# Two fp16 weight parts under a scale computed on the chip, one semaphore for both scan inputs, and a first step without recurrent passes, in a two-LSTM kernel

## The reference

```
def lstm(x, h0, Wx, Wh, b):            # _L0_cond_ref and _L0_cond2_ref, c0 = 0
    xp = einsum('ntd,df->ntf', x, Wx) + b
    for t in range(128):
        a = xp[:, t] + h @ Wh                       # 16 x 512
        i, f, o = sigmoid(a[:, :H]), sigmoid(a[:, H:2H]), sigmoid(a[:, 2H:3H])
        g = tanh(a[:, 3H:])
        c = f * c + i * g
        h = o * tanh(c)                             # kept for every t
attn(y)  = ((y Wtheta^T)(y Wphi^T)^T / sqrt(128)) (y Wg^T)     # linear, no softmax
x = x + attn(lstm(x, cond, Wx1, Wh1, b1))
x = x + relu(lstm(x, cond, Wx2, Wh2, b2) W1 + bb1) W2 + bb2
```

## Time and profile before

| | us |
|---|---|
| median of three runs | 469.54 (469.51 to 469.75) |
| the profiled execution, its own time | 466.24 |
| its span, first to last instruction | 464.2 |
| busy: TensorE / VectorE / ScalarE / GpSimd | 441.4 / 261.0 / 212.0 / 17.1 |

### The profile page before, as it was taken

The page is one execution under the profiler, slowest core; times in us unless marked ns, Lnnn a source line. Parts: engine busy times, 40 slices in busy tenths (PEclk is TensorE's granted clock), DMA queues, the critical chain, the costliest instruction groups (busy, mean ns, idle before and its releaser), DMA issues.

```text
span 464.2 us, 17097 instructions
## 1 busy us (share of the span) xinstructions
PE 441.4 (95%) x6350; PEld 351.3 (76%) x6440; DVE 261.0 (56%) x1422; ACT 212.0 (46%) x1092; POOL 17.1 (4%) x29
## 2 busy tenths in 40 slices
PE   7999999999999999999999999999999999999997
PEld 5877777777777777777789977777777777777775
DVE  4455555555555555555545656556656656665664
ACT  1444455554455555445535344444444444444443
POOL 6800000000000000000000000000000000000000
PEclk9999999999999999999999999999999999999999
DMA  5001111100111110010000000000000000000000
GB/s 168 7 3 18 17 17 17 17 12 5 17 17 17 17 17 9 8 17 11 11 13 3 7 20 20 17 17 14 3 17 17 17 17 17 11 6 17 17 17 11
DMA packets 11689, 8.12 MB, mean 17 GB/s; under 512 B 1097, under 2 KB 11129, under 8 KB 11674
## 3 DMA queue, kind: packets, MB, share of 16 engines
q1 hardware_dynamic: 10874, 6.17, 6.7%
q0 software_dynamic: 512, 1.22, 0.8%
q10 hardware_dynamic: 288, 0.52, 0.3%
HBM read 2.87 MB, written 1.05 MB: 8 GB/s over the span
## 4 chain that ended last, share of the span: by engine, by line
PE 75%; DVE 11%; ACT 9%; issue 3%; DMA 1%; ACTq 0%; DVEq 0%
PE fobank L389 19%; PE gibank L379 16%; PE fobank L379 9%; DVE cell L752 6%; ACT scan L667 5%; DVE ring L755 4%; ACT cell L674 4%; PE gibank L354 3%; PE gibank L359 3%; PE fobank L354 3%; PE fobank L359 3%; PE bankV L365 2%; PE bankY L533 2%; PE bankV L443 2%; PE bankU L526 2%
## 5 line engine op out<-in xcount | busy, mean ns | idle before, releaser
L389 PEld LDWEIGHTS fobank<-ring,whf 128*128 128x128 f32 x510 | 76.6, 189 | 77.8 <-DVE ring L755 70.3
L664 ACT ACTIVATE fgate<-fobank 128x16 f32<-128x16 f32 x256 | 46.9, 183 | 165.0 <-PE fobank L389 162.7
L389 PE MATMUL fobank<-ring,whf 128*128 128x16 f32 x510 | 99.8, 271 | 15.1 <-DVE ring L755 13.1
L748 DVE TENSOR_TENSOR scan<-fgate,cell 128x16 f32<-128x16 f32 x256 | 45.3, 177 | 86.8 <-ACT fgate L664 84.7
L752 DVE TENSOR_TENSOR_SCAN cell<-scan 128x48 f32<-128x48 f32 x256 | 68.4, 267 | 36.8 <-ACT scan L667 1.3
L379 PEld LDWEIGHTS gibank<-h_hi,wh_parts 128*128 128x128 bf16 x1536 | 78.9, 110 | 0.0
L755 DVE SCALAR_TENSOR_TENSOR ring<-cell,ogate 128x16 f32<-128x16 f32 x256 | 44.6, 174 | 59.9 <-ACT cell L674 59.9
L379 PE MATMUL gibank<-h_lo,wh_parts 128*128 128x16 f16 x1536 | 75.3, 169 | 0.3 <-DVE h_lo L760 0.2
L379 PE MATMUL gibank<-h_hi,wh_parts 128*128 128x16 f16 x1536 | 75.4, 169 | 0.0
L667 ACT ACTIVATE scan<-gibank 128x32 f32<-128x32 f32 x256 | 54.8, 214 | 28.7 <-PE gibank L379 0.8
L379 PE MATMUL fobank<-h_hi,wh_parts 128*128 128x16 f16 x771 | 60.0, 174 | 0.4 <-ACT fgate L664 0.2
(11 more groups left out here) (150 smaller groups left out, 463.2 us busy)
## 6 DMA issues: line engine op xcount, KB each, us to landing
rows_t<-rows SPq DMA_DIRECT2D x16, 128.0 KB
x_rows<-in_x_dram SPq DMA_DIRECT2D x17, 64.0 KB
out_dram<-y_sb SPq DMA_DIRECT2D x16, 64.0 KB
xres<-x2T SPq DMA_DIRECT2D x15, 64.0 KB, 1.9
xin<-x2T SPq DMA_DIRECT2D x14, 64.0 KB, 1.8
w<-in_L_ffn_W_dram POOLq DMA_DIRECT2D x2, 256.0 KB, 3.9
wh<-in_L_cond_Wh_dram ACTq DMA_DIRECT2D x1, 256.0 KB, 2.8
wx<-in_L_cond_Wx_dram ACTq DMA_DIRECT2D x1, 256.0 KB, 3.8
```

The source lines that it names most:

```text
L389: nc.tensor.matmul(step_out(p, t, GF), whf[layer][:], ring[:, (s - 1) % STEPS, :], start=False, stop=True, skip_group_check=True).then_inc ...
L664: nc.scalar.activation(fgate[:], fobank[p][:, NB * t:NB * t + NB], ACT.Sigmoid).then_inc(f_done[layer], 1)
L748: nc.vector.tensor_tensor(out=fc_slots, in0=fgate[:], in1=c_psum, op=ALU.mult).then_inc(fc_done[layer], 1)
```

## The change

- `passes` runs over **two** float16 parts of Wh instead of three bfloat16 parts: 4 passes a gate instead of 6.
- So that they fit float16's exponents, Wh is divided by a power of two and multiplied by 2^13. The power of two is found on the chip from the largest |Wh|: VectorE reduces each partition's row, TensorE spreads the 128 maxima to all partitions by a product with a diagonal matrix, VectorE takes the maximum and keeps its exponent bits. It yields four values a layer in `scale[layer]`, one column each.
- All of PSUM's pre-activations therefore carry this factor and H_UNIT: x, the bias (or the ones beside it) and h0 are multiplied by it beforehand, and ScalarE takes it out again: the scale of the three gate activations is now a column of `scale[layer]` (a 128 x 1 tile) where it was a constant.
- ScalarE's tanh of g and i and VectorE's fgate * c both count on one semaphore, `scan_inputs`, and the scan waits once, for 2n + 2.
- Step 0 of each layer has no recurrent passes: `initial` (layer 1) and `project_gate` (layer 2) signal f_ready, gi_ready and o_ready themselves. Layer 1's first 16 steps are now written out and its loop is Fori(1, ITER).
- Layer 2's scale is made between the steps of layer 1: VectorE after steps 8, 9 and 12, TensorE after step 12. GpSimd then scales wx, bias, h0 of layer 2 and splits Wh in four instructions (before: six).

```diff
-        wh_parts = [sb(f"wh_parts{n}", [P, 3, 4 * H], bf16) for n in (1, 2)]
+        wh_parts = [sb(f"wh_parts{n}", [P, 2, 4 * H], f16) for n in (1, 2)]
...
             if layer == 0:
-                e.scalar_tensor_tensor(out=rest[:], in0=w[:], scalar=1.0 / H_UNIT, in1=parts[:, 0, :],
+                eng.wait_ge(done, 2)
+                e.scalar_tensor_tensor(out=parts[:, 1, :], in0=w[:], scalar=w_scale(layer), in1=parts[:, 0, :],
                                        op0=ALU.mult, op1=ALU.subtract).then_inc(done, 1)
             else:
...
-            eng.wait_ge(done, 3 + layer)
-            e.tensor_copy(parts[:, 1, :], rest[:]).then_inc(done, 1)
-            eng.wait_ge(done, 4 + layer)
-            e.tensor_tensor(out=parts[:, 2, :], in0=rest[:], in1=parts[:, 1, :], op=ALU.subtract).then_inc(done, 1)
...
+            def top_product(layer, out):
+                pe.wait_ge(scale_made[layer], 2)
+                nc.tensor.matmul(out, ones[:], w_diag[:], start=True, stop=True).then_inc(top_ready[layer], 1)
...
                     for g in gs:
-                        for part in range(3):
+                        for part in range(2):
...
-            nc.tensor.matmul(bankV[:, 0:2 * P], warm_w[:], zeros[:], start=True, stop=True, skip_group_check=True)
-            pe.wait_ge(bias_ready, 1)
-            for g in GATES:
-                bias_gate(0, 0, g)
             pe.wait_ge(cond_loaded, 16)
             nc.tensor.transpose(bankY[:, 0:NB], cond_rows[:], ident[0:NB, 0:NB]).then_inc(cond_transposed, 1)
-            pe.wait_ge(xT_kept, 1)
-            pe.wait_ge(wx_ready, 1)
-            for g in GATES:
-                project_gate(0, 0, g, xT[:, 0, :])
+            keep_warm(bankV, 2)
+            top_product(0, gibank[1][:, 0:P])
             pe.wait_ge(h0_kept, 1)
-            pe.wait_ge(wh_ready, 1)
-            initial(0)
-
             pe.wait_ge(attn_w_loaded, 48)
             nc.tensor.matmul(bankY[:, 0:P], wtp[:, 1, :], wtp[:, 0, :], start=True, stop=True)
             nc.tensor.matmul(bankY[:, 2 * P:3 * P], wtp[:, 0, :], wtp[:, 1, :], start=True, stop=True)
             nc.tensor.transpose(bankY[:, P:2 * P], wg_rows[:], ident[:]).then_inc(proj_ready, 1)
-            pe.wait_ge(parts_ready[0], 5)
+            nc.tensor.matmul(bankV[:, 0:2 * P], warm_w[:], zeros[:], start=True, stop=True, skip_group_check=True)
+            pe.wait_ge(bias_ready, 1)
+            pe.wait_ge(ones_z_ready, 1)
+            for g in GATES[0:3]:
+                bias_gate(0, 0, g)
+                if g == GF:
+                    pe.wait_ge(xT_kept, 1)
+                    pe.wait_ge(wx_ready, 1)
+                project_gate(0, 0, g, xT[:, 0, :])
+                if g == GF:
+                    pe.wait_ge(h0_ready, 1)
+                    pe.wait_ge(wh_ready, 1)
+                last = initial(0, g)
+                if g == GF:
+                    last.then_inc(f_ready[0], 1)
+            last.then_inc(gi_ready[0], 1)
+            pe.wait_ge(f_done[0], 1)
+            bias_gate(0, 0, GO)
+            project_gate(0, 0, GO, xT[:, 0, :])
+            initial(0, GO).then_inc(o_ready[0], 1)
...
+            for s in range(STEPS):
+                if s > 0:
+                    if s == 1:
+                        pe.wait_ge(parts_ready[0], PARTS[0])
+                    step(0, s, s)
+                if s == 13:
+                    pe.wait_ge(scale_made[1], 3)
+                beside1(0, s)
+                if s == 12:
+                    top_product(1, bankU[:, 2 * P:3 * P])
+            with pe.Fori(1, ITER) as i:
...
-            for g in GATES:
-                last = project_gate(1, 0, g, x2T[:, 0, :])
-            last.then_inc(x2_projected, 1)
-            pe.wait_ge(parts_ready[1], 6)
+            project_gate(1, 0, GF, x2T[:, 0, :]).then_inc(f_ready[1], 1)
+            project_gate(1, 0, GG, x2T[:, 0, :])
+            project_gate(1, 0, GI, x2T[:, 0, :]).then_inc(gi_ready[1], 1)
+            pe.wait_ge(f_done[1], 1)
+            project_gate(1, 0, GO, x2T[:, 0, :]).then_inc(o_ready[1], 1)
...
                 nc.scalar.activation(fgate[:], fobank[p][:, NB * t:NB * t + NB],
-                                     ACT.Sigmoid).then_inc(f_done[layer], 1)
+                                     ACT.Sigmoid, scale=z_of(layer)).then_inc(f_done[layer], 1)
...
-                                     ACT.Tanh, scale=0.5).then_inc(gi_done[layer], 1)
+                                     ACT.Tanh, scale=z_half(layer)).then_inc(scan_inputs[layer], 1)
...
-                                     ACT.Sigmoid).then_inc(tanh_done[layer], 1)
+                                     ACT.Sigmoid, scale=z_of(layer)).then_inc(tanh_done[layer], 1)
...
                 nc.vector.tensor_tensor(out=fc_slots, in0=fgate[:], in1=c_psum,
-                                        op=ALU.mult).then_inc(fc_done[layer], 1)
-                dve.wait_ge(gi_done[layer], n1)
-                dve.wait_ge(fc_done[layer], n1)
+                                        op=ALU.mult).then_inc(scan_inputs[layer], 1)
+                dve.wait_ge(scan_inputs[layer], n * 2 + 2)
...
+            def most_of(layer, loaded):
+                dve.wait_ge(loaded, 16)
+                nc.vector.tensor_reduce(w_most[layer][:], wh[layer][:], axis=mybir.AxisListType.X, op=ALU.max,
+                                        apply_absolute_value=True).then_inc(scale_made[layer], 1)
+            def spread_most(layer):
+                dve.wait_ge(scale_made[layer], 1)
+                nc.vector.tensor_scalar(w_diag[:], ident[:], w_most[layer][:], LEAST, ALU.mult,
+                                        ALU.max).then_inc(scale_made[layer], 1)
+            def scale_from(layer, top):
+                dve.wait_ge(top_ready[layer], 1)
+                nc.vector.tensor_reduce(w_top[:], top, axis=mybir.AxisListType.X, op=ALU.max
+                                        ).then_inc(scale_made[layer], 1)
+                ...   # and with the exponent mask, times units, xor, times units: four instructions on 1 to 2 columns
...
+            for s in range(STEPS):
+                step(0, s, s)
+                beside1(0, s)
+                if s == 8:
+                    most_of(1, wh2_loaded)
+                if s == 9:
+                    spread_most(1)
+                if s == 12:
+                    scale_from(1, bankU[:, 2 * P:3 * P])
```

More of the change, by code:

```diff
@@ L201, in build, with z_of, z_half, w_scale @@
         out_tb = out.rearrange("b (c t) d -> c t b d", t=CH)
+        def z_of(layer):
+            return scale[layer][:, 0:1]
+        def z_half(layer):
+            return scale[layer][:, 1:2]
+        def w_scale(layer):
+            return scale[layer][:, 2:3]
+        def x_scale(layer):
+            return scale[layer][:, 3:4]
         def split_wh(eng, e, layer):
-            done, w, parts, rest = parts_ready[layer], wh[layer], wh_parts[layer], wh_rest[layer]
-            e.tensor_scalar(whf[layer][:], w[:, gate_cols(GF)], 1.0 / H_UNIT, None, ALU.mult).then_inc(done, 1)
@@ L211, in split_wh @@
                                        op0=ALU.mult, op1=ALU.subtract).then_inc(done, 1)
             else:
[L213 removed]
+                e.tensor_scalar(wh_rest[:], w[:], w_scale(layer), None, ALU.mult).then_inc(done, 1)
                 eng.wait_ge(done, 3)
[L215 to L216 removed]
@@ L217, in split_wh @@
-            e.tensor_copy(parts[:, 1, :], rest[:]).then_inc(done, 1)
-            eng.wait_ge(done, 4 + layer)
-            e.tensor_tensor(out=parts[:, 2, :], in0=rest[:], in1=parts[:, 1, :], op=ALU.subtract).then_inc(done, 1)
-        def start_h(layer):
-            nc.vector.memset(h_hi[:, STEPS - 1, :], 0.0).then_inc(hi_ready[layer], 1)
-            nc.vector.memset(h_lo[:, STEPS - 1, :], 0.0).then_inc(lo_ready[layer], 1)
+                e.tensor_tensor(out=parts[:, 1, :], in0=wh_rest[:], in1=parts[:, 0, :],
+                                op=ALU.subtract).then_inc(done, 1)
@@ L225, in start_h, with clear_c, at @@
+        PARTS = [3, 4]
+        def clear_c(layer):
             nc.vector.memset(c_psum, 0.0).then_inc(c_cleared, 1)
             nc.vector.wait_ge(c_cleared, layer + 1)
+        def at(eng, value):
+            return value if isinstance(value, int) else eng.snap(value)
         @block.sync
@@ L352, in bias_gate @@
             def bias_gate(layer, p, g):
-                return nc.tensor.matmul(gate_out(p, g), bias[layer][:, gate_cols(g)], moving(ones[:, :], g),
+                return nc.tensor.matmul(gate_out(p, g), bias[layer][:, gate_cols(g)],
+                                        moving((ones_z, ones)[layer][:, :], g),
                                         start=g in (GF, GG), stop=False, skip_group_check=True)
```

255 lines of the change are left out of this document (158 added, 97 removed).

## The result

The changed kernel takes 549.62 us (median of four runs, 548.56 to 566.81), the kernel before 469.52 (468.03 to 469.75, four runs beside them): a ratio of 1.1706 [1.1669, 1.1744]. All ratios, with 95% intervals in brackets, are made from the executions within 1.5% of the fastest of their kernel, here without the one of 566.81. I had written 467.2. The profiled execution took 550.2 us, its span 548.1, against 464.2 before.

The account below looks back on a forecast made before the run. No engine is full; the step is pure latency. Steady steps -2.6, TensorE-bound steps +0.4, layer 2's step 0 -0.5, start -0.2, layer 2's scale +0.6 sum to -2.3: 469.54 becomes 467.2 us, range 463.5 to 475.

Parts of the forecast that it names:

- rival C: TensorE's clock falls with six passes fewer a step; ten steps at the lower level cost about 5 us; chance 0.05.
- second mark: Sign of a fallen TensorE clock in the trace: the passes would start 0.05 us apart.
- GpSimd's part: GpSimd's preparation of layer 2's weights during layer 1: claimed to have 200 us of cover.
- One semaphore: 0: The scan's wait: two waits cost no more than one, so merging gains 0; bound 0.04 us a step.
- My 11 ns a step: Steady steps: 100 ns from fewer passes less 89 for the column; 237 steps give -2.6 us.
- Passes: TensorE's passes for g and i: 12 become 8, so their gates come 0.100 us earlier a step; alone 23.7 us.
- Column: ScalarE's gate activations: a column as scale instead of a constant costs 89 ns, between 0 and twice 89.
- Rival A: ScalarE's scale column is free, so the whole 0.100 us a step comes through: 445 us; chance 0.10.
- Handover: Layer 2's step 0, now without recurrent passes: its tanh of g and i starts earlier, -0.5 us.
- TensorE-bound steps: About ten steps early in layer 2, where TensorE is the bound: each 0.04 us longer, +0.4 us.
- layer 2's scale inside layer 1: VectorE's reductions and waits between layer 1's steps: +0.6 us, between 0.2 and 1.5.
- The start: Layer 1's step 0 with scale making and reordered input products: -0.2 us, between -1.5 and +2.

Follow-up runs that it names:

- 11: Changed kernel with three passes a gate again (second part used twice) in layer 2's first 16 steps alone: 470.5 us.
- 16: Changed kernel with the fill in layer 1's first 16 steps alone: 548.47 us.
- 10: Changed kernel with the fill everywhere but in layer 2's first 16 steps: 469.14 us.
- experiment 4: Kernel before with a 128 x 1 column as scale of its three gate activations, all passes kept: 495.86 us.
- 3: Kernel before with its third bfloat16 part left out of the passes, constants as scales: 460.42 us.
- 15: Changed kernel with constants as the three gate scales, nothing else added: 441.61 us.
- Experiment 5: Changed kernel with the fill in TensorE's pause before gate o's passes in every step, added into columns nothing reads: 463.07 us.
- 2: Changed kernel with three passes a gate again in every step, the second part used twice: 488.29 us.
- 6: Changed kernel with the fill in every step and two semaphores before the scan again: 479.28 us.
- 9: Changed kernel with the fill in layer 2's first 16 steps alone: seen twice, 466.95 and 536.8 us.
- 13: Changed kernel with the fill in layer 2's first 16 steps alone, timed again in more rounds: 470.52 us.
- experiment 12: Kernel before with one merged semaphore for both scan inputs: 464.12 us.
- the fill: Two extra TensorE products of 256 columns on constants, which nothing waits for, added to the changed kernel; in every step, 463.07 us.
- experiment 7: Changed kernel with the fill in every step and constants as the three gate scales, right for these weights alone: 442.86 us.
- 14: Changed kernel with the fill in every step, placed behind gate o's passes instead of in the pause before them: 465.38 us.
- 8: Changed kernel with the fill in the first 16 steps of each layer alone, none in the loops: 465.1 us.

## Why the prediction was wrong

**The step that failed is rival C, its chance and its price.** The mechanism was named, with the right mark to look for (a granted clock under 1.00), and put at 0.05 and ten steps. Its second mark, passes 0.05 apart, is not in the trace: the 16-column passes start 0.027 us apart at the lower level and 0.025 at the higher, and it is the 128-column products that go from 0.11 to 0.21. Measured: 11 steps at the lower level in layer 1, near what ten were priced at (+6.3), and then all of the last 117, +78.7, which I didn't consider. Two sentences carried the mistake.

- "The passes removed are 16 columns each, very little of the array's work." Experiments 11 and 16 are the same in layer 2 but for those passes in 15 steps, and 11 holds where 16 falls. That a granted clock of 1.00 over the whole record left a margin was assumed; no row said how large it was, and a row of 1.00 can't.
- "If the lower of the two levels (1.2 GHz) held for ten steps it would cost about 10 x 0.5 = 5 us". It was priced as an episode, and at 0.5 us a step, where the row it quotes (2.46 against 1.70) gives 0.76 and 0.67 was measured. At the lower level the recurrent step is bound by TensorE, 2.36 instead of 1.69 us, so the same products are spread over 40% more time; that a recovery must follow was never argued. In layer 1 it followed after 24 us. In the kernel before it always did: of its 68 executions timed beside the experiments, 26 have a mean clock of 0.996 or less (0.996 is some 3.7 us at the lower level), the lowest 0.95, and none takes over 482 us. The one trace at 1.00 that I read was of an execution without such a dip. In layer 2 only extra work brought it (10) or the third passes, which experiment 4 still has.

**What starts the fall** is narrowed down for layer 2, though on two executions for most of the kernels: it is the first 16 steps, through the six passes fewer each and the longer ScalarE instructions together. Each alone only dips (3 and 4), and with constant scales (15) the level of layer 2 holds even without the passes. In layer 1 it is less sharp. The level fell at 46.3, after the steps 13, 14 and 18 had each grown. Timeline of the changed kernel around step 13:

```profile
33.94 0.29 DVE L836 TENSOR_REDUCE w_top<-bankU 128x1 f32<-128x128 f32 x1
...
34.78 0.23 DVE L847 TENSOR_SCALAR scale<-units,w_inv 128x2 f32<-128x2 f32 x1
34.92 0.17 DVE L872 TENSOR_TENSOR scan<-fgate,cell 128x16 f32<-128x16 f32 x1
...
35.87 0.28 PE L434 MATMUL fobank<-ring,whf 128*128 128x16 f32 x1 [0.55 <-DVE ring L878]
...
36.83 0.57 DVE L875 TENSOR_TENSOR_SCAN cell<-scan 128x48 f32<-128x48 f32 x1
...
42.46 1.15 POOL L251 TENSOR_TENSOR wh_parts<-wh_rest,wh_parts 128x512 f16<-128x512 f32 x1
...
43.16 0.48 DVE L883 TENSOR_TENSOR h_lo<-ring,h_hi 128x16 f16<-128x16 f32 x1
```

VectorE's reduction and the four small ones hold fgate * c back, and TensorE waits 0.55 us, its longest wait after the start (0.52 at the handover comes next). Experiment 5 has the same two waits, 0.55 and 0.52, and holds the level, so they don't take it down by themselves. GpSimd can begin its share of layer 2's weights only when the scale is there, so it works from 35.11 to 43.61, and two of VectorE's instructions beside it are stretched: the scan to 0.57 from 0.27, h_lo to 0.48 from 0.18. I had given GpSimd's part 200 us of cover and no price. Experiments 2, 6, 9, 11, 13, 15 and 16 dip there too, between 37 and 55 us, and the traces of the kernel before and of experiment 12 don't. But 6 and 16 have the fill in these steps and dip for 3.4 us in spite of it: what starts the fall in layer 1 stays open.

**"One semaphore: 0" was wrong as a value and harmless as a sum.** I argued from a scan whose second input comes 0.11 us after the first. In the changed step both come within 0.02 us, and there two waits cost 0.058 us (6), 237 x 0.058 = 14 us over the kernel (6 less 5 is 16.2, but 6 also wrote its first h 3.2 us later); my bound had been 0.04. In the kernel before the edit is worth nothing (12), as said. My 11 ns a step was right only because this edit was in it.

**The rest held, but for the start.** Passes: 0.100 us, by experiment 7 (1.702 - 1.601 = 0.101). Column: 0.090. Sum -0.010 a step, forecast -0.011. The Trainium skill, "ScalarE: Activation LUTs", section "What ACT_TABLE_LOAD costs", has about 93 ns for a pointer operand; for a scale these runs show 90. Rival A's time, 445, is what experiment 7 has (442.86), because there the column isn't read. Handover -0.3 (forecast -0.5), TensorE-bound steps +0.3 (+0.4), layer 2's scale inside layer 1 +1.3 for steps 9 to 18 (+0.6, within 0.2 to 1.5). The start was -1.7 instead of -0.2: the first h was written at 12.89 instead of 14.63. That gain is luck, not the new order. The changed kernel's trace reached the higher level 9 us sooner. Experiment 12, the kernel before but for one semaphore, reached it at 7.8 us and wrote its first h at 12.03; experiment 5 did at 8.4 and 12.86. Like for like the new start is 0.8 us longer, and the spans of the two traces, 460.4 and 461.1 us, put the worth of the change at the higher level at 0.7 us (the medians, 463.07 beside 464.72, at 1.7), under the 2.3 I had added up.

**Open.** Why one of fourteen executions with the fill in layer 2's first steps fell; it left no trace, and of such an execution only the mean clock is known, not where the level was low. And how much work a stretch must have, and of which measure: the experiments say which of two kernels holds, not where the border lies. The version with the fill is faster than the changed kernel, and than the kernel before by 0.45% (0.9955 [0.9922, 0.9988]); the one with constant scales is the fastest run here, and is only right while the weights' largest value stays in the same power of two.

## What to carry to other kernels

A latency-bound loop that rests on the array's higher level has a margin that the profile of a granted clock of 1.00 doesn't show: before passes are taken out of it, find the thinnest stretch, and price the loss as lasting, at the loop's length times the difference of the two steps (here 117 x 0.67 us). If work must go, put products on constants where no one waits for them (here 2 x 256 columns a step, at no cost in the step) and see whether the time changes. Give inputs that end together one semaphore, and keep the scale of a ScalarE instruction on the critical path a constant where it can be one.

## What the runs showed of the hardware

- The level fell with no long pause of the array before it: 252 to 261.3 has 8.60 us of TensorE's busy time in 9.30, and after the start no wait of TensorE in the whole trace is over 0.55 us. The Trainium skill, "TensorE: Matmul & The Clock Gate", section "HAM oscillation — how this bites in real kernels", ties the fall to idle gaps of microseconds while a kernel waits for DMA; no such gap is in this trace, and 14 shows the level held with the pause left as it was. Here more products held it, wherever in the step they stood.
- The level that a loop runs at can be kept by the loop itself: the same 112 steps held the higher one in experiments 8, 11 and 13 and the lower one in the changed kernel and in 16.
- The time at which the level first rose differed from run to run, from 7.8 us (12) to 42 (4).
- The lower level doesn't slow narrow products: 16-column passes start 0.027 us apart there and 0.025 at the higher level, 128-column float32 products 0.21 and 0.11, 512-column bfloat16 ones 0.43 and 0.22.
- GpSimd stretches VectorE: 0.27 to 0.57 and 0.18 to 0.48 us in the rows of 36.83 and 43.16. In all eighteen traces every scan over 0.30 us and every h_lo over 0.21 overlaps an instruction of GpSimd, in the kernel before too (h_lo 0.63 us at 19.43).
- A VectorE instruction behind two semaphore waits started at least 0.10 us after the end of VectorE's instruction before it; behind one wait, 0.03 to 0.05 us (experiments 3 and 6 against 5 and the changed kernel).
- A ScalarE instruction of 128 x 16 or 128 x 32 takes 0.09 us longer with a column as scale, and fgate's extra 0.09 doesn't hold back the tanh behind it: they start 0.20 apart with 0.27 of duration.
